# The first layer of a two-layer network as one stream of 64 pairs of heads, with every score formed twice and the softmax weights split on POOL and DVE

## The chip, the cores and the metric

The kernel runs on one core of a Trainium2 chip. Five engines share the work, each with its own queue of instructions in fixed order: PE (TensorE, matmuls and transposes, which write only to the eight PSUM banks), DVE (VectorE), ACT (ScalarE), POOL (GpSimd, which here touches only SBUF), and SP (SyncE), which issues the transfers. They meet through semaphores: an instruction waits until a counter has reached a value. The metric is the device time of one execution in microseconds (us), as the median of several.

## What is computed

Input x has 4 batches of 512 rows of 512 elements. Only the first layer (attention and a linear map, each with a layer norm before and after) is touched by the change; a second layer follows and stays as it is.

```
x = hidden_states                                   # (4, 512, 512), fp32
# first layer, attention: 32 heads of 16, one shared key and value head
n1 = layernorm(x);  q = n1 @ Wq;  k, v = n1 @ Wkv   # k, v: 16 wide
scores = q.k / 4 + slope[h] * (key_pos - query_pos), masked where key > query
x = x + layernorm((softmax(scores) @ v) @ Wo)
# first layer, linear map with 8-bit codes and scales
x = x + layernorm(layernorm(x) @ W.T + bias)
# then the second layer: attention with 32 heads of 128, and a gated feed-forward
```

## The kernel before

Products of fp32 data are formed from fp16 halves: a = hi + lo, and hi·hi + lo·hi + hi·lo is accumulated, so each use costs three matmuls, and each operand needs an instruction that makes hi (mostly ACT) and one that makes lo = a - hi (mostly DVE).

`layer0` works in rounds. `run(b, attend, back, front)` is one round: it attends batch b, carries the back part of batch b-1 (product with Wo, norms, linear map) and the front part of batch b+1 (norm and transposes). The rounds are run(-1) and run(4) without attention, run(0), a loop over run(1) and run(2), and run(3). Each ends with a barrier of all engines.

In a round the 32 heads go one at a time (h = 0..31). For head h, PE forms the scores of four tiles of 128 queries against the keys up to their own (1280 columns in all, `scores`, L459). DVE adds the distance bias from table `tab` and takes the row maximum in one instruction per tile (`biased`, L680), POOL makes `tab` for the head (L371), ACT exponentiates in SBUF (L575) with the row maximum as bias. PE then transposes the 10 blocks of weights (`transpose_probs`, L472), since the product with the values needs the keys on the partitions; ACT copies them to fp16 `pT_hi` (L543), DVE forms `pT_lo` (L708), and PE multiplies 10 blocks by the values in three terms (`weigh_values`, L484). A column of ones in the values gives the sum of each row, by which DVE divides at the start of the next round (L649, L652).

The order on PE is written out: in step h it transposes head h-1, stacks queries, weighs the values for head h-2, forms the scores of head h+1, and then does what `extra` puts there (products with Wq, Wo and the linear weights; transposes n1, n2, n3). The eight PSUM banks are a ring in the order of `uses`: a fill waits until the use eight places earlier has been emptied (`take`). On DVE step h is `biased_scores(h)`, then lo of the extras and of head h-1, then norms. The scores with bias lie in `xp`, four heads deep, and the fp16 weights three heads deep.

## Time and profile before

| | us |
|---|---|
| median of 3 runs | 2516.77 |
| lowest, highest | 2516.7, 2525.8 |
| profiled execution, its time | 2520.12 |
| profiled execution, span of the core | 2518.3 |

The profile is of one execution; its span starts with the first instruction and ends with the last, 1.8 us short of that execution's own time. The first layer lies from 58.97 us (DVE's first scalar) to 823.7 us (the last of its transposes is out). PE is busy 85% of the whole span, DVE 74%, ACT 61%, POOL 27%. A row of the form "L680 DVE ... x128 | 95.1, 743 | 4.3 <-PE" is a group: its line, engine and operation, what it writes and reads, how many; then its busy time in us and the mean ns of one; then the idle time before its members and what ended it. In a timeline a row has the start, the length (of all its members together where it says x4), and in brackets the idle time before it. PEclk in a stretch is the granted TensorE clock as a share of 2.4 GHz.

### The profile page before, as it was taken

How to read it: one execution, taken by the hardware profiler on the slowest of the kernel's cores; microseconds unless marked ns; L12 is line 12 of the kernel's file. 1: busy time of each engine (PE TensorE's matmuls, PEld its weight loads, DVE VectorE, ACT ScalarE, POOL GpSimd, SP SyncE). 2: the span in 40 equal slices, each digit the busy share in tenths (PEclk: the TensorE clock that was granted, in tenths of full speed). 3: DMA queues.
4: the chain of work that ended last, by engine and by line, in shares of the span. 5: the costliest groups of instructions: out<-in, count | busy, mean ns of one | idle time of the engine just before them, and what ended most of it. 6: DMA issues, size and time to landing. Idle time of an engine off the chain costs nothing. (4 is left out here: it accounts for less than half of the span.)

```text
span 2518.3 us, 49756 instructions
## 1 busy us (share of the span) xinstructions
PE 2146.9 (85%) x18352; PEld 1310.3 (52%) x18352; DVE 1864.5 (74%) x4645; ACT 1531.5 (61%) x3606; POOL 688.4 (27%) x563
## 2 busy tenths in 40 slices
PE   6688777778774589999999999999999999758997
PEld 2465555555552255555555555655555556423443
DVE  3688897897995477777777777777777777575554
ACT  2587776777771376667667676667666767341221
POOL 0312212111110243343433343334333333112221
PEclk9899899889997799999999999999999999978999
DMA  5101001000000343444334434443344333320000
GB/s 203 33 2 35 1 7 47 2 18 18 2 18 17 115 81 63 89 87 91 80 66 89 81 71 82 80 91 78 64 89 84 66 68 65 72 87 17 34 17 34
DMA packets 380593, 147.59 MB, mean 59 GB/s; under 512 B 354928, under 2 KB 359664, under 8 KB 378304
## 3 DMA queue, kind: packets, MB, share of 16 engines
q1 hardware_dynamic: 380352, 144.41, 25.5%
q8 instruction: 147, 2.41, 0.4%
q14 instruction: 94, 0.77, 0.1%
HBM read 48.95 MB, written 11.53 MB: 24 GB/s over the span
## 5 line engine op out<-in xcount | busy, mean ns | idle before, releaser
L1157 ACT ACTIVATE xp<-xp,nm 128x128 f32<-128x128 f32 (+3 forms) x512 | 281.3, 550 | 354.5 <-DVE nm L1236 354.5
L1017 POOL TENSOR_TENSOR q_in_sbuf<-q_in_sbuf,sinq 128x512 f32<-128x512 f32 x128 | 231.2, 1806 | 688.2 <-ACT q_in_sbuf L1145 581.3
L1207 DVE SCALAR_TENSOR_TENSOR probs_lo<-xp,rl,probs_hi 128x128 f16<-128x128 f32 (+3 forms) x512 | 263.5, 576 | 109.4 <-ACT probs_hi L1122 109.4
L575 ACT ACTIVATE xp<-xp,nm 128x512 f32<-128x512 f32 (+3 forms) x512 | 249.8, 569 | 50.9 <-DVE nm L680 49.1
L680 DVE CUSTOM_DVE_ANT_0 xp<-bank,tab,cs 128x512 f32<-128x512 f32 (+3 forms) x512 | 250.2, 545 | 4.3 <-PE bank L459 2.0
L1236 DVE CUSTOM_DVE_ANT_0 xp<-bank,mask,cs 128x128 f32<-128x128 f32 (+3 forms) x512 | 250.3, 545 | 0.0
L1122 ACT ACTIVATE probs_hi<-xp,rl 128x128 f16<-128x128 f32 (+3 forms) x512 | 244.0, 549 | 0.7 <-DVE rl L1256 0.7
L472 PE MATMUL bank<-ident,xp 128*128 128x128 f32 x1280 | 182.7, 291 | 62.6 <-ACT xp L575 45.6
L1041 PE MATMUL bank<-xT_hi,wq_hi 128*128 128x512 f16 x512 | 195.2, 381 | 43.2 <-DVE yacc L1251 37.4
L708 DVE TENSOR_TENSOR pT_lo<-bank,pT_hi 128x384 f16<-128x384 f32 (+1 forms) x384 | 207.1, 593 | 32.5 <-ACT pT_hi L543 32.4
L1041 PE MATMUL bank<-p1T_hi,v_hi 128*128 128x128 f16 x1280 | 223.0, 220 | 2.9 <-DMA p1T_lo<-probs_lo 2.9
L1041 PE MATMUL bank<-p1T_hi,v_lo 128*128 128x128 f16 x1280 | 222.9, 220 | 0.0
L1041 PE MATMUL bank<-p1T_lo,v_hi 128*128 128x128 f16 x1280 | 222.8, 220 | 0.0
L543 ACT ACTIVATE pT_hi<-bank 128x384 f16<-128x384 f32 (+1 forms) x384 | 181.0, 537 | 57.0 <-PE bank L472 55.0
L1024 POOL TENSOR_TENSOR qf<-q_in_sbuf,t 128x512 f32<-128x512 f32 x160 | 204.3, 1277 | 31.2 <-POOL q_in_sbuf L1017 19.0
L472 PEld LDWEIGHTS bank<-ident,xp 128*128 128x128 f32 x1280 | 150.4, 148 | 99.9 <-issue 27.9
L371 POOL TENSOR_SCALAR tab<-rel,cinv 128x512 f32<-128x512 f32 x128 | 92.5, 725 | 390.0 <-DVE nm L680 318.3
L1041 PE MATMUL bank<-xT_hi,wq_lo 128*128 128x512 f16 x512 | 195.2, 381 | 0.0
L1041 PE MATMUL bank<-xT_lo,wq_hi 128*128 128x512 f16 x512 | 195.0, 381 | 0.0
L1041 PE MATMUL bank<-wo_hi,o1T_hi 128*128 128x512 f16 x512 | 194.0, 379 | 1.1 <-issue 1.1
L1041 PE MATMUL bank<-wo_lo,o1T_hi 128*128 128x512 f16 x512 | 194.0, 379 | 0.0
L1041 PE MATMUL bank<-wo_hi,o1T_lo 128*128 128x512 f16 x512 | 194.0, 379 | 0.0
(235 smaller groups left out, 5535.9 us busy)
## 6 DMA issues: line engine op xcount, KB each, us to landing
raw_q<-in_wq SPq DMA_DIRECT2D x8, 1024.0 KB, 5.3
raw_o<-in_wo SPq DMA_DIRECT2D x8, 1024.0 KB, 5.6
x_front<-in_x SPq DMA_DIRECT2D x4, 1024.0 KB, 5.8
xb<-in_x SPq DMA_DIRECT2D x4, 1024.0 KB, 7.1
x_scratch<-xb SPq DMA_DIRECT2D x4, 1024.0 KB, 4.4
x_before<-x_scratch SPq DMA_DIRECT2D x4, 1024.0 KB, 5.6
wup<-in_wup SPq DMA_DIRECT2D x3, 1024.0 KB, 11.9
fused_scratch<-fused SPq DMA_DIRECT2D x12, 256.0 KB, 2.4
```

The source lines that it names most:

```text
L472: last = pe.transpose(bank[:, at:at + P], xp[:, h % 4, TRI[t] + j * P:TRI[t] + (j + 1) * P], C["ident"][:, :])
L543: act.activation(pT[0][:, h % 3, COLD[js[0]]:COLD[js[0]] + n, :], bank_of(("T", h, i))[:, 0:n * P].rearrange("p (t c) -> p t c", c=P), ACT ...
L575: act.activation(x, x, ACT.Exp, scale=-1.0, bias=nm[:, h % 4, t:t + 1]).then_inc(s_ex, 1)
L680: ins = dve.tensor_tensor_reduce(out=xp[:, h % 4, TRI[t]:TRI[t] + w], in0=bank_of(u)[:, at:at + w], in1=tab[:, h % 4, S - w:S], scale=cs[: ...
L708: dve.tensor_tensor(pT[1][:, h % 3, c, :], bank_of(u)[:, 0:n * P].rearrange("p (t c) -> p t c", c=P), pT[0][:, h % 3, c, :], ALU.subtract) ...
L1017: pool.tensor_tensor(qs[:, i % 2, :], qs[:, i % 2, :], rope["sink" if u[0] == "k" else "sinq"][:, :], ALU.mult).then_inc(s_rot, 1)
L1024: pool.tensor_tensor(qf[:, i % 2, :], qs[:, i % 2, :], t2[:, i % 2, :], ALU.add).then_inc(s_qf, 1)
L1041: ins = pe.matmul(out, lhs(a), rhs(c), start=(first and i == 0), stop=(last and i == 2))
L1122: ins = act.activation(pr[0][:, m % 2, c], xp[:, m % 3, c], ACT.Copy, scale=rl[:, m % 3, t:t + 1])
L1157: ins = act.activation(x, x, ACT.Exp, scale=-1.0, bias=nm[:, m % 3, t:t + 1], accum_out=ls[:, m % 3, t:t + 1])
L1207: ins = dve.scalar_tensor_tensor(pr[1][:, m % 2, c], xp[:, m % 3, c], rl[:, m % 3, t:t + 1], pr[0][:, m % 2, c], ALU.mult, ALU.subtract)
L1236: ins = dve.tensor_tensor_reduce(out=xp[:, m % 3, TRI[t]:TRI[t] + w], in0=bank_of(("s", m, i))[:, col:col + w], in1=mask[:, S - w:S], scal ...
```

## The change

The rounds go. All 4 x 16 = 64 pairs of heads pass through one stream of steps n, written out without a loop or a barrier; step n belongs to all engines.

- Scores are formed twice. A pair's scores go to five PSUM banks with queries on the partitions (`scores`, L544), only for their row maxima (`maximise`, five reductions on DVE). Six steps later they are formed again with keys on the partitions (`exponents`, L573), the maximum and the distance bias included as extra rows of the operands `q_stack` and `k_stack`, and ACT exponentiates straight from PSUM (`exponentials`, 5 x 128x512). So there is no transpose of weights, no `tab`, no `stack`. Blocks not computed or half masked are covered by matmuls of a constant (`mask_scores`, `mask_exponents`).
- The weights, 128x2560 fp32 for a pair in `px` (two deep), are split on POOL (`weights_hi`, one cast) and DVE (`weights_lo`, one subtraction). PE weighs the values in 40 small matmuls a pair.
- Queries are stacked by 24 transfers of 16x512 for every four pairs, maxima by 4 transfers, all issued by SP.
- Heads are normed on POOL (`norm_heads`, 16 small instructions for four pairs); the residual additions move from DVE to POOL (`add_rows`), the row norms from DVE and POOL to ACT (`normalise`).
- The other work hangs on steps: batch b's front and back parts lie in the steps that FRONT and BACK give, counted from 16b, and `others(n)` is filled at the end of PE's step n and emptied at the start of ACT's and DVE's step n+1.
- The banks stay one ring of eight, in the order of `fillings`.

```diff
+        X_LAG, V_LAG, N_LAG = 6, 8, 9
...
+        kz = sc.sb("k_stack_max", [P, 2, S], F16)
+        ks = sc.sb("k_stack", [P, 2, S], F16)
...
+        px = sc.sb("weights", [P, 2, 5, S])
+        ph = [sc.sb("weights_hi", [P, 2, 5, S], F16), sc.sb("weights_lo", [P, 2, 5, S], F16)]
...
+        STEPS = range(-16, NP + N_LAG + 20)
...
+        FRONT = {"load": -16, "stats": -13, "norm": -12, "n1": -10, "kv": -2}
+        BACK = {"load": 27, "o": 25, "y": (26, 27, 29, 30), "add1": 31, "n2": 33, "f": (34, 35, 37, 38),
+                "add2": 39, "n3": 42}
...
+        fillings = []
+        for n in STEPS:
+            if 0 <= n < NP:
+                fillings += [("s", n, i) for i in range(5)]
+            if 0 <= n - V_LAG < NP:
+                fillings.append(("pv", n - V_LAG))
+            if n % GP == 0 and 0 <= n // GP - 1 < NG:
+                fillings.append(("m", n // GP - 1))
+            if 0 <= n - X_LAG < NP:
+                fillings += [("x", n - X_LAG, i) for i in range(5)]
+            fillings += others(n)
+        place = {u: i for i, u in enumerate(fillings)}
...
+                def stack_queries(g):
+                    sp.wait_ge(s_qd, g + 1)
+                    if g >= GP:
+                        sp.wait_ge(*filled[("x", GP * (g - GP) + 3, 4)])
+                    else:
+                        sp.wait_ge(s_st, 2)
+                    for h in range(8):
+                        for lo, r in ((0, 16), (1, 32), (0, 48)):
+                            to = 64 * (h % 2) + r
+                            sp.dma_start(qs[to:to + E0, g % GP, h // 2, :],
+                                         qq[lo][h * E0:(h + 1) * E0, g % 2, :]).then_inc(s_qs[g % 2], 16)
...
+                def norm_heads(g):
+                    b, m = g // GP, g % GP
+                    pool.wait_ge(s_ro, g + 1)
+                    if m == 0 and b >= 1:
+                        pool.wait_ge(*last_of("o", b - 1))
+                    for h in range(8):
+                        c, o = (8 * m + h) * E0, ob[:, g % 2, h, :, :]
+                        if g or h:
+                            pool.wait_ge(s_on, 8 * g + h)
+                        pool.tensor_tensor(od[:, :, :], o[:, :, 0:E0], o[:, :, EV:EV + E0], ALU.add).then_inc(s_os, 1)
+                        pool.wait_ge(s_os, 8 * g + h + 1)
+                        pool.tensor_tensor(on[:, :, c:c + E0], od[:, :, :],
+                                           ro[:, g % 2, h, :].unsqueeze(2).to_broadcast([P, TT, E0]),
+                                           ALU.mult).then_inc(s_on, 1)
+                def weights_hi(p):
+                    pool.wait_ge(*emptied[("x", p, 4)])
+                    if p >= 2:
+                        pool.wait_ge(s_pf, p - 1)
+                    pool.tensor_copy(ph[0][:, p % 2, :, :], px[:, p % 2, :, :]).then_inc(s_wh, 1)
...
+                pool.wait_ge(s_sc, 1)
+                for n in STEPS:
+                    for u in norms_at(n):
+                        rstd(norm_no[u])
+                        if u in add_no:
+                            add_rows(u)
+                    if 0 <= n - X_LAG < NP:
+                        weights_hi(n - X_LAG)
+                    g, r = divmod(n - N_LAG - 3, GP)
+                    if r == 0 and 0 <= g < NG:
+                        norm_heads(g)
+
...
+                def take(u):
+                    i = place[u]
+                    if i >= 8:
+                        pe.wait_ge(*emptied[fillings[i - 8]])
+                    return banks[i % 8]
...
+                def mask_exponents(p):
+                    for i in range(5):
+                        out = take(("x", p, i))
+                        if i < 2:
+                            pe.matmul(out[:, 0:P], far[:, :], trit[:, 0, :], start=True, stop=False,
+                                      skip_group_check=True)
+                        else:
+                            parts = out[:, :].rearrange("p (a c) -> p a c", c=P)
+                            pe.matmul(parts[:, 0::3, :] if i < 4 else parts[:, 0::2, :], far[:, :], trit[:, :, :],
+                                      start=True, stop=False, skip_group_check=True)
+                def exponents(p):
+                    g, pp = p // GP, p % GP
+                    if pp == 0:
+                        pe.wait_ge(s_mr[g % 2], 16 * 4 * (g // 2 + 1))
+                        pe.wait_ge(s_kr, 2 * (g // GP) + 2)
+                    k = ks[:, g // GP % 2, :]
+                    for i, e, j, c in ((0, 0, 0, 0), (1, 1, 0, 0), (4, 0, 2, 0), (3, 1, 1, 0), (2, 0, 1, 0),
+                                       (3, 1, 3, 3 * P), (4, 1, 2, 2 * P), (2, 0, 3, 3 * P)):
+                        if (j, e) == (2, 1):
+                            pe.wait_ge(s_he, p + 1)
+                        r = slice(64 * e, 64 * (e + 1))
+                        ins = pe.matmul(bank_of(("x", p, i))[:, c:c + S - j * P], k[r, j * P:(j + 1) * P],
+                                        qs[r, g % GP, pp, j * P:S], start=False, stop=True, skip_group_check=True)
+                        if (j, e) == (2, 0):
+                            ins.then_inc(s_he, 1)
+                        elif j != 1:
+                            ins.then_inc(s_ef, 1)
...
+                    if 0 <= n < NP:
+                        mask_scores(n)
+                        scores(n)
+                    if 0 <= n - V_LAG < NP:
+                        weigh_values(n - V_LAG)
+                    if n % GP == 0 and 0 <= n // GP - 1 < NG:
+                        turn_maxima(n // GP - 1)
+                    if 0 <= n - X_LAG < NP:
+                        mask_exponents(n - X_LAG)
+                        exponents(n - X_LAG)
+                    for u in others(n):
+                        fill(u)
...
+                def exponentials(p):
+                    if p >= 2:
+                        act.wait_ge(s_wl, p - 1)
+                    for i in range(5):
+                        act.wait_ge(*filled[("x", p, i)])
+                        act.activation(px[:, p % 2, i, :], bank_of(("x", p, i))[:, :], ACT.Exp,
+                                       scale=unit[:, 0:1]).then_inc(s_ed, 1)
...
+                for n in STEPS:
+                    for u in others(n - 1):
+                        evacuate(u)
+                    for u in norms_at(n):
+                        normalise(u)
+                    if 0 <= n - X_LAG < NP:
+                        exponentials(n - X_LAG)
+                    if 0 <= n - V_LAG < NP:
+                        copy_heads(n - V_LAG)
...
+                def maximise(p):
+                    g, pp = p // GP, p % GP
+                    if g >= 2 and pp == 0:
+                        dve.wait_ge(*filled[("m", g - 2)])
+                    m4 = mx[:, g % 2, 0:32].rearrange("p (e a t) -> p e a t", e=2, t=TT)
+                    for i in range(5):
+                        bank = bank_of(("s", p, i))
+                        dve.wait_ge(*filled[("s", p, i)])
+                        if i < 2:
+                            ins = dve.tensor_reduce(m4[:, i, pp, 3:4], bank[:, :], AX.X, ALU.max)
+                        elif i < 4:
+                            ins = dve.tensor_reduce(mp[:, g % 2, GP * (i - 2) + pp, :],
+                                                    bank[:, :].rearrange("p (a c) -> p a c", c=P), AX.X, ALU.max)
+                        else:
+                            ins = dve.tensor_reduce(m4[:, :, pp, 1], bank[:, :].rearrange("p (a c) -> p a c", c=2 * P),
+                                                    AX.X, ALU.max)
+                        ins.then_inc(s_sd, 1)
+                def weights_lo(p):
+                    dve.wait_ge(s_wh, p + 1)
+                    dve.tensor_tensor(ph[1][:, p % 2, :, :], px[:, p % 2, :, :], ph[0][:, p % 2, :, :],
+                                      ALU.subtract).then_inc(s_wl, 1)
...
+                scalars()
+                for n in STEPS:
+                    if n % GP == 0 and 0 <= n // GP - 1 < NG:
+                        join_maxima(n // GP - 1)
+                    for u in others(n - 1):
...
+                    if 0 <= n - X_LAG - 1 < NP:
+                        weights_lo(n - X_LAG - 1)
+                    if 0 <= n < NP:
+                        maximise(n)
...
-        run(-1, False, False, True)
-        run(0, True, False, True)
-        with nc.Fori(1, B - 1) as b:
-            run(b, True, True, True)
-        run(B - 1, True, True, False)
-        run(B, False, True, False)
```

The first place is DVE's queue. Before, in a round's third step, the biased scores of one head (its second row, `nm`, is the row maximum of the same instruction), then the lo of an older head and of a query projection:

```order
L680 ISA xp,nm<-bank,tab,cs 128x512 [waits s_s_filled,s_table]
L680 ISA nm 128x1
L680 ISA xp,nm<-bank,tab,cs 128x384 [waits s_s_filled]
L680 ISA nm 128x1
L680 ISA xp,nm<-bank,tab,cs 128x128
L680 ISA nm 128x1
L708 TENSOR_TENSOR pT_lo<-bank,pT_hi 128x384 [waits s_t_hi_out] x2
L708 TENSOR_TENSOR pT_lo<-bank,pT_hi 128x512 [waits s_t_hi_out]
L644 TENSOR_TENSOR qT_lo<-bank,qT_hi 128x512 [waits s_s_hi_out]
```

And now, in step 32, with the emptying of a query projection and the statistics of the back part's rows ahead:

```order
L896 TENSOR_REDUCE mx<-mp 128x8 [waits s_scores_maximised]
L898 COPY mx<-mp 128x8 [waits s_dve_steps]
L856 SCALAR_TENSOR_TENSOR q_lo<-bank,fq,q_hi 128x512 [waits s_queries_hi]
L812 BN_STATS st<-xb 128x6 [waits s_rows_added] x4
L820 BN_AGGR mv<-st 128x2 [waits s_dve_steps,s_rows_normed]
L820 BN_AGGR mv<-st 128x2 x3
L822 TENSOR_SCALAR ve<-mv 128x4 [waits s_dve_steps]
L890 TENSOR_TENSOR weights_lo<-weights,weights_hi 128x2560 [waits s_weights_hi]
L879 TENSOR_REDUCE mx<-bank 128x1 [waits s_scores_filled,s_maxima_transposed]
L879 TENSOR_REDUCE mx<-bank 128x1 [waits s_scores_filled]
L881 TENSOR_REDUCE mp<-bank 128x4 [waits s_scores_filled] x2
L884 TENSOR_REDUCE mx<-bank 128x2 [waits s_scores_filled]
```

Where the lo followed the maxima of a newer head, the one lo of a pair (L890, waiting for POOL) now stands ahead of the five maxima of the pair seven steps younger.

The second place is PE's queue around the product with the values. Before, transposes, the stacking of queries, and the product:

```order
L472 MATMUL bank<-ident,xp 128x128 [waits s_exp,s_s_freed_by_dve]
L472 MATMUL bank<-ident,xp 128x128 x2
L472 MATMUL bank<-ident,xp 128x128 [waits s_exp,s_t_lo_out]
L472 MATMUL bank<-ident,xp 128x128 x3
L443 MATMUL bank<-qT_hi,sel 128x512 [waits s_s_freed_by_dve,s_t_lo_out]
L444 MATMUL bank<-qT_lo,sel 128x512
L484 MATMUL bank<-v,pT_hi 128x17 [waits s_t_lo_out]
```

Now, behind the product with the values of a pair:

```order
L555 MATMUL bank<-tri_T,far 128x128 [waits s_exponentials] x2
L559 MATMUL bank<-tri_T,far 128x2x128 [waits s_scores_maximised] x3
L573 MATMUL bank<-q_stack,k_stack 128x512 x2
L573 MATMUL bank<-q_stack,k_stack 128x256
L573 MATMUL bank<-q_stack,k_stack 128x384 x2
L573 MATMUL bank<-q_stack,k_stack 128x128
L573 MATMUL bank<-q_stack,k_stack 128x256 [waits s_half_of_exponents_filled]
L573 MATMUL bank<-q_stack,k_stack 128x128
L524 MATMUL bank<-tri,far 128x128 [waits s_scores_maximised] x2
L527 MATMUL bank<-tri,far 128x256 [waits s_pv_out]
```

The transposes are gone; the second forming of the scores (L573) stands behind mask fills (L559) that take banks from the maxima of this same step.

The third place is POOL. Before it made tables and, in rounds with a front part, normed four row tiles:

```order
L371 TENSOR_SCALAR tab<-rel,cinv 128x512 [waits s_s_freed_by_dve] x2
L359 TENSOR_TENSOR rs<-ve,mhalf 128x4 [waits s_variance]
L363 TENSOR_SCALAR x_front<-x_front,mv,rs 128x512 [waits s_rstd]
L363 TENSOR_SCALAR x_front<-x_front,mv,rs 128x512 x3
L371 TENSOR_SCALAR tab<-rel,cinv 128x512 [waits s_s_freed_by_dve] x6
```

Now, in the steps in which batch 0's rows are added:

```order
L458 TENSOR_TENSOR rs<-ve,mhalf 128x4 [waits s_rows_normed,s_variance]
L460 TENSOR_TENSOR nb<-mv,rs 128x4 [waits s_rstd]
L462 TENSOR_SCALAR nb<-nb 128x4 [waits s_rstd]
L491 TENSOR_TENSOR xb<-xb,yb 128x512 [waits s_rows_normed,s_x_loaded]
L491 TENSOR_TENSOR xb<-xb,yb 128x512 [waits s_rows_normed] x3
L483 CAST weights_hi<-weights 128x2560 [waits s_pv_filled,s_exponentials]
```

POOL used to work ahead of the heads; its cast now stands between ACT's exponentials and DVE's lo of every pair.

## Rows read from the trace of the kernel before

**Rows 1.** Stretches of the first layer: length, busy per engine, PEclk, DMA share, GB/s.

```profile
core 0: us, PE busy (x) PEld busy (x) DVE busy (x) ACT busy (x) POOL busy (x), PEclk, DMA share, GB/s
400.70:580.00 179.30, 142.49 (x1652) 100.50 (x1653) 157.15 (x452) 126.34 (x296) 34.16 (x39) 0.89 0.06 19
757.00:830.00 73.00, 33.70 (x170) 20.25 (x166) 39.52 (x81) 10.15 (x17) 4.04 (x4) 0.71 0.10 33
```

**Rows 2.** Waits from 400 to 579 us: waiter, who ended it, us, times, longest.

```profile
POOL tab L371 <- DVE nm L680: 78.5, 20, 16.2
...
ACT xp L575 <- DVE nm L680: 17.0, 8, 6.6
```

**Rows 3.** Groups on POOL, whole span.

```profile
L1024 POOL TENSOR_TENSOR qf<-q_in_sbuf,t 128x512 f32<-128x512 f32 x160 | 204.3, 1277 | 31.2 <-POOL q_in_sbuf L1017 19.0 <-DVE t L1223 7.6
L371 POOL TENSOR_SCALAR tab<-rel,cinv 128x512 f32<-128x512 f32 x128 | 92.5, 725 | 390.0 <-DVE nm L680 318.3 <-POOLq L96 69.4
...
L363 POOL TENSOR_SCALAR x_front<-x_front,mv,rs 128x512 f32<-128x512 f32 x12 | 24.8, 2082 | 0.3
...
L1826 POOL MEMSET mhalf<- 128x8 f32 x1 | 0.1, 105 | 0.3 <-POOLq L1940 0.3
```

**Rows 4.** Groups on DVE, whole span.

```profile
L680 DVE CUSTOM_DVE_ANT_0 xp<-bank,tab,cs 128x512 f32<-128x512 f32 x128 | 95.1, 743 | 4.3 <-PE bank L459 2.0 <-PE bank L472 1.4 <-POOL tab L371 0.7
L1215 DVE TENSOR_TENSOR q1T_lo<-qf,q1T_hi 128x512 f16<-128x512 f32 x128 | 87.6, 684 | 13.8 <-ACT q1T_hi L1136 13.6
...
L170 DVE TENSOR_TENSOR raw_wf<-raw_wf,qscales 128x2048 f32<-128x2048 f32 x1 | 2.3, 2293 | 0.0
L172 DVE TENSOR_REDUCE w_am<-raw_wq 128x1 f32<-128x2048 f32 x1 | 2.3, 2287 | 11.8 <-DMA raw_wq<-in_wq 11.8
```

**Rows 5.** DVE's timeline, first tens of microseconds.

```profile
14.00 0.74 DVE L172 TENSOR_REDUCE w_am<-raw_wkv 128x1 f32<-128x576 f32 x1
```

**Rows 6.** Groups on ACT, whole span.

```profile
L575 ACT ACTIVATE xp<-xp,nm 128x512 f32<-128x512 f32 x128 | 93.8, 733 | 47.7 <-DVE nm L680 47.7
...
L575 ACT ACTIVATE xp<-xp,nm 128x128 f32<-128x128 f32 x128 | 51.8, 405 | 0.0
...
L1560 ACT ACTIVATE silu_gate<-bank_g,tern_scale 128x512 f32<-128x512 f32 x40 | 27.5, 688 | 144.7 <-PE bank_g L1515 144.6
```

**Rows 7.** ACT's timeline, a head's four exponentials behind the copy of `stk`.

```profile
483.65 0.59 ACT L535 ACTIVATE stk<-bank 128x512 f16<-128x512 f32 x1
484.14 1.90 ACT L575 ACTIVATE xp<-xp,nm 128x512 f32<-128x512 f32 x4
```

**Rows 8.** PE's timeline: 128x512 matmuls at half clock, and later at full.

```profile
79.18 0.63 PE L398 MATMUL bank<-front_T_hi,wkv_lo 128*128 128x512 f16 x1
79.61 0.63 PE L398 MATMUL bank<-front_T_lo,wkv_hi 128*128 128x512 f16 x1
...
482.96 0.38 PE L443 MATMUL bank<-qT_hi,sel 128*128 128x512 f16 x1
483.17 0.38 PE L444 MATMUL bank<-qT_lo,sel 128*128 128x512 f16 x1
```

**Rows 9.** SP's timeline: two transfers of 64 KB issued.

```profile
844.81 1.23 SPq L1000 DMA_DIRECT2D raw_kv<-in_wkr  x2
```

**Rows 10.** DVE's timeline in the last round: first, some statistics, last.

```profile
758.73 0.95 DVE L649 RECIPROCAL rsum<-ob 128x128 f32<-128x128 f32 x1 [2.13 <-PEq L96]
...
776.49 2.47 DVE L592 BATCH_NORM_STATS2 st<-yb 128x6 f32<-128x512 f32 x4 [10.99 <-ACT yb L563]
...
822.98 0.69 DVE L639 TENSOR_TENSOR xT_lo<-bank,xT_hi 128x512 f16<-128x512 f32 x1 [0.16 <-ACT xT_hi L512]
```

**Rows 11.** Second layer's timeline: POOL's additions with DVE's subtraction beside them.

```profile
2271.30 6.03 POOL L1459 TENSOR_TENSOR yacc<-x_before,normed 128x512 f32<-128x512 f32 x4 [1.27 <-DVE normed L1593]
...
2271.81 1.31 DVE L1724 TENSOR_TENSOR hidden_lo<-hidden,hidden_hi 128x512 f16<-128x512 f32 x1
```

935 lines of the change are left out of this document (497 added, 438 removed).

## The prediction

> **What bounds the kernel now.** I read the stretches of the first layer first. A steady round is 179.3 us, that is 11.2 us for each of its 16 pairs of heads with everything else included. DVE is busy for 157.15 of it, PE for 142.49, ACT for 126.34, POOL for 34.16 [rows 1]. Then the waits of that stretch: POOL waits for DVE 78.5 us, ACT waits for DVE 17.0 [rows 2], while DVE, before its 128 biggest instructions, stood idle 4.3 us in all [rows 4]. So DVE sets the pace and the others work beside it, buffered three or four heads deep. The reader is to see two things: what takes work off DVE could pay, and 11.2 us a pair is the mark that the new stream has to beat. More exactly: the layer ends at 823.7 us. Its end in the new kernel is a start, 57 periods of the step, and a run-out. With start and run-out as worked out below, the new kernel breaks even at a period of 9.9 us.
>
> **What the change takes and adds, by load.** Off PE go the transposes and the stacking of queries, on comes the second forming of the scores with its masks, 3584 columns a pair: at the pace of 0.21 us for 512 columns [rows 8] that is 1.5 us; and the product with the values is 40 matmuls of 34 columns, 0.6 by columns. PE has room. ACT loses the copies of transposed weights and gets five exponentials of full width. DVE's load a pair becomes one lo of 2560 columns, five reductions and its share of the other work. By length, DVE's one row of this kind (2293 ns for 2048 columns, against 684 for 512) gives 1.05 ns a column, so 2.83 us; a reduction is 2287 ns for 2048 [rows 4] and 0.74 us for 576 [rows 5], so 0.673 us for 512, five make 3.37. The other work of a batch is some 20 emptyings and lo of 0.69, three statistics of 2.47 and some 0.5 [rows 10], and about 17 of keys, values, maxima and row sums: 39 us, 2.44 a pair. DVE's load is thus 8.6 us a pair, below 11.2. By load alone the change wins. The question is whether load or a chain of waits sets the step.
>
> **The chain of a step.** Read the order of the three engines together. In step n, DVE's queue has `weights_lo(n-7)` ahead of `maximise(n)`. PE's mask fills for `exponents(n-6)` take, in the ring of eight, the banks that stand eight places earlier: those of the pair's last ones are the first three score banks of pair n, the same step. So they wait for three reductions of `maximise(n)`. Behind the masks come the exponents, then ACT's five exponentials, then POOL's one cast, which waits for the fifth, then DVE's `weights_lo(n-6)`, which waits for the cast and stands ahead of `maximise(n+1)`. The circle closes in one step, and no buffer in it can get ahead: two deep in `px` doesn't help, since the exponents themselves wait for the maxima. The period is therefore the sum of the links:
>
> - PE, from the last maximum to ACT's first start: a mask and the first product. Before, ACT's copy of `stk` starts 0.69 us after PE's first of two matmuls of 512 columns at full clock [rows 7, 8]; at half clock these follow each other at 0.43 instead of 0.21 [rows 8], which makes 1.1 to 1.2. I take 0.9.
> - ACT, five of 128x512 from PSUM: such a one is 0.688; from SBUF 0.733 at 512 columns and 0.405 at 128 [rows 6]. The four of a head together (1280 columns) take 1.90 though their means sum to 2.28 [rows 6, 7]: each gives 0.12 back to overlap. 5 x 0.688 less 4 x 0.12 is 3.0.
> - POOL, a cast of 128x2560, fp32 to fp16, of one input. No row has such a cast. The nearest is `tab`, one input and 512 columns: 0.725 [rows 3]. A fixed part of 0.105, the smallest POOL row [rows 3], leaves 0.62 for 512; five of these and the fixed part are 3.2, I take 3.1. Upper bounds: the two-input product, 1.277 x 5 = 6.4, and the one-input row with two scalars, 2.08 x 5 = 10.4 [rows 3]. Lower: the slope of ACT's exponentials, (0.733 - 0.405) / 384 = 0.85 ns a column [rows 6], gives 2.3 with the fixed part, say 2.4. A gain is excluded, since the cast starts only when ACT's fifth is out and lo only when the cast is out. I stay at 3.1, since `tab` is nearest in kind.
> - DVE, lo of 2560 columns: 2.83. Then the three reductions: 2.02. In every fourth step the turned maxima take a bank of the ring and a fourth reduction counts: 0.17 on average.
> - Handing over between engines, five times beyond what the links hold: 0.15 in all.
>
> Sum: 0.9 + 3.0 + 3.1 + 2.83 + 2.02 + 0.17 + 0.15 = 12.2 us. PE's own work and ACT's emptyings fall into the 8.9 us of ACT, POOL and lo, and are hidden; if PE ran at half clock throughout, they would just fill it.
>
> The Trainium skill (GPSIMD Engine Reference, sections 3.1 and 4.1) says that an operation with one input is roughly at line rate on GpSimd, 1.03 cycles an element. The row of `tab` does not agree: 0.725 for 512 columns is well above. By that rule the cast would be an estimated 2.2 us and the period 11.3.
>
> **What comes on top of the chain.** Instructions in DVE's queue ahead of lo are free as long as they end before POOL's cast does: after the maxima DVE has the links of PE, ACT and POOL, 7.0 us, less the two last reductions, so some 5.7 us. Steps with little fit in. Those with emptyings, statistics of four row tiles (3 us) and reciprocals do not, because what they wait for arrives late or lies behind each other: of 16 steps, seven carry such work (n mod 16 = 0, 4, 7, 8, 11, 12, 15), with an excess of 1 to 3 us. Four batches: between 40 and 70 us, I take 55. The 24 transfers with which SP stacks queries for four pairs take 24 x 0.62 = 15 us by SP's row (two in 1.23) [rows 9] out of 49 for four steps, so they are hidden. Where POOL norms eight heads in 16 small instructions, it does so just beside lo. In the second layer a DVE subtraction of two SBUF operands beside POOL's additions took 1.31 [rows 11] against 0.684 in general [rows 4]. Lo lengthened by 0.34 to 0.9 of itself in 14 or 15 steps is 14 us. The sum on top: 69.
>
> The Trainium skill (SBUF — State Buffer, Who interferes with whom) says that a DVE instruction with two SBUF inputs contends with a GpSimd instruction that reads SBUF and that the later one waits for the whole of the other. The trace agrees with the contention (1.31 against 0.684). Lo mostly starts first; by that rule it would lose at most one small POOL instruction each time, and the 14 us would be about 5.
>
> **Start and run-out.** From 58.97: norm of batch 0 some 20 (with the load), transposes and first queries 8, the 24 transfers and their landing 17, six steps of scores alone at 5 reductions each, 3.4, so 20, and stacking the maxima 6: 71, first exponents at 130. After the last maxima the chain runs six pairs more without scores (6 x 5.5), the last heads are normed (8 x 3), and the back part of batch 3 follows. That back part took from 758.73 to 823.7 before, 65 [rows 10], at a PEclk of 0.71 [rows 1], and I take the same; part of the six pairs lies beside norming, so 33 + 24 + 65 = 122, with handing over 130.
>
> **The forecast.** 130 + 57 x 12.2 + 69 + 130 = 1024 us for the end of the layer, against 823.7: 200 us longer. The profiled execution's own 2520.12 becomes 2720.8; its median is 3.35 lower, so 2717. The second layer and the preparation are untouched.
>
> **Rivals.**
> (A) The chain as above, 2717; with the links off by 8% (56 us) and the extras by 20, 2640 to 2790. For it: the three orders; the row of `tab`. Chance 0.62.
> (B) The cast is dear, near the two-input rate: 3.3 us more in each period is 188, of which 40 come back because the extras then fit: 2865. At 10.4 for the cast it would be 3093. For it: the spread of POOL's rows between one shape and another (0.725 to 2.08). Against: `tab` is nearer in kind. Chance 0.15.
> (C) The cast at 2.4, PE's link 0.7 and extras of 42: a period of 11.3, end at 130 + 644 + 42 + 130 = 946, time 2639; with start and run-out each 20 shorter, 2600. Chance 0.13. The skill's rate for the cast, named above, would lead here.
> (D) Faster: the fills of the exponents do not in fact wait for the maxima of the same step, so that ACT and POOL get a pair ahead of DVE, and DVE's load of 8.6 us is the period: 130 + 57 x 8.65 + 130 = 753, time 2446. It decides where the mean step is below 9.9 us. Against it: the ring's order, which puts three score banks of the same step under the exponents' masks; DVE idle ahead of lo would have to be near nothing. Chance 0.07. That both nearly cancel (a mean step of 9.7 to 10.1) has 0.03.
>
> **How the numbers follow.** The likeliest is A, 2717. The range takes A, most of C and B up to its middle value: 2590 to 2860. Within 0.5%, about what a measurement of this kernel can tell from no change, 0.03; faster 0.07; slower 0.90, from A, B and C.
>
> **What would show it.** Of the changed kernel's profile: a steady step of some 13.4 us (12.2 and 1.2 of extras); POOL's cast at a mean near 3.1; DVE idle ahead of lo, ended by POOL, some 4 us a step, and DVE busy for 65% of the stream; PE's mask fills (L559) ended by DVE's reductions; ACT idle ended by PE; PEclk below the 0.89 of before. Wrong would be: the mask fills rarely waiting for DVE (then D), a cast beyond 5 us (B), or a start or run-out of 200 us instead of 130, which the first and last of L890 show at once.

## The result, and the profile after

The changed kernel takes 2711.65 us (median of 4 runs, 2706.31 to 2716.75) against 2520.28 of the kernel before. The ratio is 1.0757, with a 95% interval of 1.0725 to 1.0789. The forecast was 2717. The last transposes of the first layer are out at 1019.96 us instead of 823.67. From there to the end it is 1695.0 us, against 1694.6 before, so the second layer is what it was, and all but 0.4 of the 196.7 us that the span grew (2715.0 less 2518.3) lie in the first layer.

Its stretches, in the columns of [rows 1]: the start up to the first exponential, the first steps, the steady stream, and the steps without scores, then the last back part.

```profile
core 0: us, PE busy (x) PEld busy (x) DVE busy (x) ACT busy (x) POOL busy (x), PEclk, DMA share, GB/s
58.97:141.00 82.03, 36.51 (x213) 16.35 (x215) 42.37 (x110) 20.74 (x34) 4.96 (x42) 0.61 0.12 39
141.00:229.00 88.00, 54.04 (x527) 25.99 (x521) 49.75 (x59) 29.27 (x54) 25.75 (x24) 0.62 0.06 13
229.00:880.00 651.00, 433.72 (x3997) 211.67 (x3998) 382.06 (x523) 234.64 (x421) 268.83 (x295) 0.68 0.07 19
880.00:926.90 46.90, 27.13 (x324) 15.37 (x322) 26.77 (x23) 24.34 (x45) 27.89 (x29) 0.68 0.01 2
926.90:1021.00 94.10, 41.70 (x259) 26.09 (x257) 36.37 (x76) 29.95 (x47) 34.37 (x60) 0.71 0.09 34
```

In the steady stream no engine is near full: DVE 59%, PE 67%, ACT 36%, POOL 41%, where DVE had 88% in [rows 1]. The granted clock of PE is 0.68 instead of 0.89. Every engine has time to spare here, so they must be waiting for each other. The timeline of one step, all engines, shows that they do so in a circle. Columns are the start, the length, engine, line and tiles, and in brackets the idle time before and what ended it.

```profile
189.89 2.32 POOL L483 CAST weights_hi<-weights 128x2560 f16<-128x2560 f32 x1 [8.84 <-ACT weights L726]
...
192.24 2.83 DVE L890 TENSOR_TENSOR weights_lo<-weights,weights_hi 128x2560 f16<-128x2560 f32 x1 [5.34 <-POOL weights_hi L483]
...
194.99 1.28 DVE L879 TENSOR_REDUCE mx<-bank 128x1 f32<-128x512 f32 x2
...
195.73 0.39 PE L559 MATMUL bank<-tri_T,far 128*128 128x256 f16 x1 [2.14 <-DVE mx L879]
196.19 1.27 DVE L881 TENSOR_REDUCE mp<-bank 128x4 f32<-128x512 f32 x2
...
196.32 0.40 PE L559 MATMUL bank<-tri_T,far 128*128 128x256 f16 x1 [0.20 <-DVE mx L879]
...
196.92 0.39 PE L559 MATMUL bank<-tri_T,far 128*128 128x256 f16 x1 [0.20 <-DVE mp L881]
...
197.25 1.27 PE L573 MATMUL bank<-q_stack,k_stack 64*128 64x512 f16 x8
...
197.98 3.00 ACT L726 ACTIVATE weights<-bank,unit 128x512 f32<-128x512 f32 x5 [7.87 <-PE bank L573]
...
201.05 2.32 POOL L483 CAST weights_hi<-weights 128x2560 f16<-128x2560 f32 x1 [8.84 <-ACT weights L726]
...
203.40 2.83 DVE L890 TENSOR_TENSOR weights_lo<-weights,weights_hi 128x2560 f16<-128x2560 f32 x1
```

Read it from lo to lo: 192.24 lo, 194.99 maxima (2.75), 196.83 third maximum out (1.84), 197.98 exponentials (1.15), 201.05 cast (3.07), 203.40 lo (2.35): 11.16 us, and the links hardly overlap. Such a step, with nothing late ahead of lo, is called clean below. The three mask fills L559 each start right behind one of DVE's reductions: they are the link that the order of the ring makes. The waits of the whole stream (141 to 880 us: waiter, who ended it, us, times, longest) say the same in sums:

```profile
POOL weights_hi L483 <- ACT weights L726: 392.0, 53, 13.8
ACT weights L726 <- PE bank L573: 346.3, 47, 9.6
PEld bank L559 <- DVE mx L879: 133.2, 100, 3.3
...
DVE q_lo L856 <- ACT q_hi L701: 63.6, 13, 5.7
...
DVE weights_lo L890 <- POOL weights_hi L483: 52.4, 20, 5.3
```

POOL waits for ACT, ACT for PE, PE for DVE and DVE for POOL: in [rows 2] the arrows led to DVE only. The groups of the page give the sizes:

```profile
L726 ACT ACTIVATE weights<-bank,unit 128x512 f32<-128x512 f32 x320 | 191.7, 689 | 362.8 <-PE bank L573 362.8
...
L483 POOL CAST weights_hi<-weights 128x2560 f16<-128x2560 f32 x64 | 148.4, 2320 | 409.4 <-ACT weights L726 409.4
...
L890 DVE TENSOR_TENSOR weights_lo<-weights,weights_hi 128x2560 f16<-128x2560 f32 x64 | 183.8, 2871 | 65.1 <-POOL weights_hi L483 64.9
```

The 57 periods from the first lo (147.03) to the 58th (881.73) sum to 734.7 us, a mean of 12.89. Against 57 x 11.15 that leaves 99 us of extras. Followed step by step in the timeline, 79 of them lie between the end of the cast and the start of lo, in steps in which something late stands ahead of lo on DVE, as in this one, where PE forms queries and a tile of the linear map:

```profile
496.97 1.27 PE L573 MATMUL bank<-q_stack,k_stack 64*128 64x512 f16 x8
...
497.71 3.00 ACT L726 ACTIVATE weights<-bank,unit 128x512 f32<-128x512 f32 x5 [9.08 <-PE bank L573]
...
500.77 2.32 POOL L483 CAST weights_hi<-weights 128x2560 f16<-128x2560 f32 x1 [10.05 <-ACT weights L726]
...
501.94 0.69 ACT L701 ACTIVATE q_hi<-bank,fq 128x512 f16<-128x512 f32 x1 [0.94 <-PE bank L516]
...
502.66 0.75 DVE L856 SCALAR_TENSOR_TENSOR q_lo<-bank,fq,q_hi 128x512 f16<-128x512 f32 x1 [4.42 <-ACT q_hi L701]
...
504.53 0.75 DVE L865 SCALAR_TENSOR_TENSOR yb<-bank,gm,bias 128x512 f32<-128x512 f32 x1 [1.12 <-PE bank L516]
...
505.92 2.45 DVE L812 BATCH_NORM_STATS2 st<-x_front 128x6 f32<-128x512 f32 x4
...
508.97 2.82 DVE L890 TENSOR_TENSOR weights_lo<-weights,weights_hi 128x2560 f16<-128x2560 f32 x1
```

The cast is out at 503.1, yet lo starts at 508.97. DVE idled 4.42 us for the queries and 1.12 for the product, and then did the statistics that could have been done in the idle time, but stand behind it.

Another 16 us lie ahead of ACT's exponentials, in 11 steps like the next one:

```profile
509.14 3.54 POOL L458 TENSOR_TENSOR rs<-ve,mhalf 128x4 f32<-128x4 f32 x1 [6.05 <-DVE ve L822]
...
512.90 1.28 DVE L881 TENSOR_REDUCE mp<-bank 128x4 f32<-128x512 f32 x2
...
513.32 2.92 ACT L718 ACTIVATE x_front<-x_front,nb,rs 128x512 f32<-128x512 f32 x4 [10.69 <-POOL nb L462]
...
516.15 2.97 ACT L726 ACTIVATE weights<-bank,unit 128x512 f32<-128x512 f32 x5
```

POOL's row factor starts beside lo (508.97) and takes 3.54 us instead of the 1.04 that it takes alone (last section). ACT's row norm waits for it and stands ahead of the exponentials, which start 2.6 us behind the third maximum instead of 1.15. The remaining 4 us are small delays at the same place where the turned maxima take a bank.

### The profile page after: what moved, and what is told of

Its sections match the earlier page's. It is cut to its first block and busy times, and to the rows that moved or that the text cites. A ratio compares the mean times of both kernels' runs of the same rounds, so it can differ in the third digit from the quotient of the medians.

```text
span 2715.0 us, 44950 instructions
## 1 busy us (share of the span) xinstructions
PE 2167.9 (80%) x16896; PEld 1202.4 (44%) x16896; DVE 1761.9 (65%) x3602; ACT 1359.9 (50%) x3014; POOL 913.7 (34%) x851
## 5 line engine op out<-in xcount | busy, mean ns | idle before, releaser
L726 ACT ACTIVATE weights<-bank,unit 128x512 f32<-128x512 f32 x320 | 191.7, 689 | 362.8 <-PE bank L573 362.8
L483 POOL CAST weights_hi<-weights 128x2560 f16<-128x2560 f32 x64 | 148.4, 2320 | 409.4 <-ACT weights L726 409.4
L890 DVE TENSOR_TENSOR weights_lo<-weights,weights_hi 128x2560 f16<-128x2560 f32 x64 | 183.8, 2871 | 65.1 <-POOL weights_hi L483 64.9
L1224 PE MATMUL bank<-xT_lo,wq_hi 128*128 128x512 f16 x512 | 196.7, 384 | 0.0
L559 PE MATMUL bank<-tri_T,far 128*128 128x256 f16 x192 | 69.4, 373 | 127.1 <-DVE mx L879 111.0
L1224 PE MATMUL bank<-kT_hi,q1T_hi 128*128 128x128 f16 (+3 forms) x512 | 148.5, 303 | 18.9 <-DVE q1T_lo L1398 18.2
L1224 PE MATMUL bank<-kT_hi,q1T_lo 128*128 128x128 f16 (+3 forms) x512 | 154.9, 303 | 0.0
L1224 PE MATMUL bank<-kT_lo,q1T_hi 128*128 128x128 f16 (+3 forms) x512 | 154.8, 302 | 0.0
```

Source lines behind the costliest of these rows:

```text
L483: pool.tensor_copy(ph[0][:, p % 2, :, :], px[:, p % 2, :, :]).then_inc(s_wh, 1)
L559: pe.matmul(parts[:, 0::3, :] if i < 4 else parts[:, 0::2, :], far[:, :], trit[:, :, :], start=True, stop=False, skip_group_check=True)
L726: act.activation(px[:, p % 2, i, :], bank_of(("x", p, i))[:, :], ACT.Exp, scale=unit[:, 0:1]).then_inc(s_ed, 1)
L890: dve.tensor_tensor(ph[1][:, p % 2, :, :], px[:, p % 2, :, :], ph[0][:, p % 2, :, :], ALU.subtract).then_inc(s_wl, 1)
L1224: ins = pe.matmul(out, lhs(a), rhs(c), start=(first and i == 0), stop=(last and i == 2))
```

## The experiments

The first six alter one thing each in the changed kernel; those under the last heading build on the first of them. Times are medians; a ratio is to the kernel before, run beside it.

**Lo behind the maxima.** This takes lo and cast out of the circle and leaves every load as it is.

```diff
-                    if 0 <= n - X_LAG - 1 < NP:
-                        weights_lo(n - X_LAG - 1)
                     if 0 <= n < NP:
                         maximise(n)
+                    if 0 <= n - X_LAG - 1 < NP:
+                        weights_lo(n - X_LAG - 1)
```

> On DVE, the lo of pair n-7 goes behind the five maxima of pair n instead of ahead of them; nothing else changes. Theory of the circle (maxima of the same step, masks, exponents, exponentials, cast, lo, next maxima): POOL's cast and DVE's lo drop out of the circle, and the step is set by load. DVE's load in the changed kernel's steady stretch is 382 us for 50.5 steps, 7.6 a step, PE's 434, 8.6 a step at its granted clock of 0.68. With some waits a step of about 9 instead of 12.9: 57 x 3.9 = 222 us less, some 2490 us (2450 to 2560), under the kernel before. Rival (the loads themselves, PE at half clock and DVE sharing SBUF with POOL, set the step): within 20 us of 2712.

Measured: 2528.07 us, ratio 1.0013 (0.9999 to 1.0026). The rival of loads is out: the same instructions in another order give back 184 of the 191 us. The mean period is 9.51 us. Here is its stretch from 229 to 700 us:

```profile
229.00:700.00 471.00, 339.02 (x3830) 182.69 (x3830) 386.01 (x503) 224.52 (x407) 256.90 (x296) 0.81 0.09 24
```

DVE is busy for 82% and PE's clock rose to 0.81 by itself. The 82% is close to the 88% of [rows 1]. The time is 38 us above the theory's central figure (2490) and inside its range.

**Exponents first in PE's step and in the ring.** The masks of the exponents then wait for the maxima of the step before.

```diff
+            if 0 <= n - X_LAG < NP:
+                fillings += [("x", n - X_LAG, i) for i in range(5)]
             if 0 <= n < NP:
                 fillings += [("s", n, i) for i in range(5)]
...
+                    if 0 <= n - X_LAG < NP:
+                        mask_exponents(n - X_LAG)
+                        exponents(n - X_LAG)
                     if 0 <= n < NP:
                         mask_scores(n)
                         scores(n)
```

> PE does the masks and exponents of pair n-6 at the start of step n, ahead of the scores of pair n, and the ring of banks has the same order; DVE's order stays (lo ahead of the maxima). The exponents' banks then come from the maxima of step n-1. Circle theory: the circle spans two steps, so it no longer binds, as in the run with lo behind: 2450 to 2580. Rival (it is DVE's order of lo before maxima that costs, whatever the ring does, or the loads): 2690 to 2720.

Measured: 2578.12 us, ratio 1.0203 (1.0183 to 1.0223). DVE's order is untouched, and still 134 us are gone: the circle needs both lo ahead of the maxima and the maxima ahead of the same step's exponents. Cut at either place it opens. The time is at the upper end of what was expected, and its waits from 300 to 750 us show what is left:

```profile
PEld bank L527 <- ACT weights L726: 102.5, 25, 11.1
```

The score masks now take banks that ACT's exponentials of the same step must empty, which is another circle.

**The cast twice.**

```diff
+                    pool.tensor_copy(ph[0][:, p % 2, :, :], px[:, p % 2, :, :]).then_inc(s_w2, 1)
+                    pool.wait_ge(s_w2, p + 1)
                     pool.tensor_copy(ph[0][:, p % 2, :, :], px[:, p % 2, :, :]).then_inc(s_wh, 1)
```

> POOL casts each pair's weights twice, the second over the first, and only the second signals DVE: 2.4 us more a pair. Circle theory: POOL's cast is a link of every step in which DVE has nothing late ahead of its lo. By the list of the 57 periods, the steps above 11.15 us that do not end in a wait for POOL have slack, and what is left is 78 us more: 2790 (2770 to 2810). If POOL's cast were hidden: 2712. If it were on the path of every step: 2850.

Measured: 2809.72 us, 98 more than the changed kernel. The 57 periods sum to 813.3 us against 734.7: 79 more, where the slack counted step by step gave 78. The estimate had left out the last six pairs, where the cast has no cover: from the 58th lo to the layer's end it is 9 us more, and the start gives 1. That makes 88 in the layer (1108.12 against 1019.96). Of the other 10 between the medians, 5 are there because the profiled execution of the changed kernel (2716.75) lies that much above its median, and 4.6 lie behind the first layer, a stretch that takes between 1693 and 1700 us in these profiles. So the cast is on the path in a part of the steps, neither hidden (0) nor always exposed (137).

**The cast in five pieces**, each as soon as its exponential is out.

```diff
-                    pool.wait_ge(*emptied[("x", p, 4)])
                     if p >= 2:
                         pool.wait_ge(s_pf, p - 1)
-                    pool.tensor_copy(ph[0][:, p % 2, :, :], px[:, p % 2, :, :]).then_inc(s_wh, 1)
+                    for i in range(5):
+                        pool.wait_ge(*emptied[("x", p, i)])
+                        pool.tensor_copy(ph[0][:, p % 2, i, :], px[:, p % 2, i, :]).then_inc(s_wh, 1)
```

> POOL casts the five banks of a pair one by one, each as soon as its exponential is out; DVE's lo waits for the fifth. Circle theory: the link between ACT's last exponential and lo shrinks from 2.32 to about 0.55 us, which counts only in the 20 or so steps in which DVE waits for POOL ahead of lo (at most 1.8 each, 31 us by the list of the waits), and in those up to the time at which the emptyings come: 2680 (2665 to 2700). If the cast is not on the path: 2712.

Measured: 2682.66 us, 29 less. The clean step is 9.4 instead of 11.15, a gain of 1.8 as expected. But only some 20 of 57 steps are clean, and the others had lost their wait for POOL already: the periods sum to 703.8, 31 less. This is the same link measured from the other side.

**Useless matmuls that keep PE busy.**

```diff
                         out = take(("s", p, i))
+                        if i == 0 and not others(p - 1):
+                            for _ in range(10):
+                                pe.matmul(out[:, :], far[:, :], oner[:, :], start=True, stop=False,
+                                          skip_group_check=True)
...
                         out = take(("x", p, i))
+                        if i == 0:
+                            for _ in range(8):
+                                pe.matmul(out[:, :], far[:, :], oner[:, :], start=True, stop=False,
+                                          skip_group_check=True)
```

> The changed kernel, with useless matmuls of 128x512 on PE, in banks that it is about to fill anyway: 10 ahead of the score masks in steps that follow no other product, 8 ahead of the exponents' masks, so that PE is not idle there; nothing of the result changes. Tests what the half clock (0.68 granted on average) is worth. Theory: PE's link in the circle goes from 1.15 to some 0.85 us and products of 12 matmuls end up to 2.5 us earlier for the emptyings that stand ahead of lo: a clock of 0.85 or more and 25 to 60 us less, 2650 to 2690. Rival (the clock costs nothing, PE has slack): 2712, or more where the added matmuls are in the way.

Measured: 2685.63 us, 26 less, at the near edge of what was expected; by the ratio to the kernel before, run beside each, it is 33 less (1.0624 against 1.0757). Its steady stretch and PE's link of a clean step:

```profile
229.00:880.00 651.00, 510.36 (x4771) 260.96 (x4772) 400.55 (x538) 248.15 (x450) 288.34 (x317) 0.91 0.07 20
```

```profile
184.70 1.27 DVE L889 TENSOR_REDUCE mp<-bank 128x4 f32<-128x512 f32 x2
...
184.84 0.28 PE L567 MATMUL bank<-tri_T,far 128*128 128x256 f16 x1 [0.31 <-DVE mx L887]
...
185.44 0.28 PE L567 MATMUL bank<-tri_T,far 128*128 128x256 f16 x1 [0.32 <-DVE mp L889]
...
185.66 0.84 PE L581 MATMUL bank<-q_stack,k_stack 64*128 64x512 f16 x8
...
186.17 3.00 ACT L734 ACTIVATE weights<-bank,unit 128x512 f32<-128x512 f32 x5 [7.54 <-PE bank L581]
```

At a granted clock of 0.91 instead of 0.68, from the third maximum (185.34) to ACT's start is 0.83 us instead of 1.15, and the clean step is 10.8. That is 0.3 in each of 57 steps, 17 or 18 us, of the 34 by which the sum of the periods fell (700.2). The rest fits products that end earlier, but wasn't measured apart. So the low clock is mostly a result of the waiting, as the clock of 0.81 with lo behind shows too; by itself it costs about 1%.

**Lo ahead of the emptyings.**

```diff
                         join_maxima(n // GP - 1)
+                    if 0 <= n - X_LAG - 1 < NP:
+                        weights_lo(n - X_LAG - 1)
                     for u in others(n - 1):
                         evacuate(u)
...
-                    if 0 <= n - X_LAG - 1 < NP:
-                        weights_lo(n - X_LAG - 1)
                     if 0 <= n < NP:
```

> The changed kernel, with DVE's lo ahead of the emptyings and statistics of its step instead of behind them, still ahead of the maxima. Tells whether the extras of some steps are work of DVE or its waiting for products of PE and ACT's halves. Steps without such work stay at 11.15. If it is mostly waiting, lo covers it: 20 to 60 us less. If it is mostly DVE work that found room while POOL was casting, that work now lies behind lo in the open: some 137 us of it against 99 of extras, 2730 to 2760. I expect the second, weakly.

Measured: 2729.6 us (two executions), at the lower edge of the second expectation. That is 18 more by the medians, but 11 by the ratio (1.0802 against 1.0757), and the periods sum to 738.3 against 734.7, only 4 more. Clean steps stay at 11.2. This fits work that now lies open behind lo in place of waits that lo now covers, which no run took apart. Between the two orders little is to be had; both put everything into one circle. As evidence on the extras it is weak, since both readings gave sums near this one.

**Versions on the way to a faster one.** All have lo behind the maxima. The first puts ACT's copy of the heads ahead of its exponentials.

```diff
-                    if 0 <= n - X_LAG < NP:
-                        exponentials(n - X_LAG)
                     if 0 <= n - V_LAG < NP:
                         copy_heads(n - V_LAG)
+                    if 0 <= n - X_LAG < NP:
+                        exponentials(n - X_LAG)
```

> As the run with lo behind the maxima, and ACT copies the heads of pair n-8 ahead of the exponentials of pair n-6 instead of behind them. In the run with lo behind, PE waited 87 us (of 300 to 750) for that copy before it could mask the next scores, so a smaller circle is left: exponentials, copy, masks and scores of the next pair, maxima, exponents; its clean step is 7.9. Theory: the copy (0.42) and its place behind 3.0 us of exponentials leave the circle, steps shorten by some 0.4 to 1 us: 2505 to 2485 against 2528. Rival (DVE's load of 82% busy already sets the step): 2520 to 2530.

Measured: 2521.41 us, ratio 0.998 (0.9971 to 0.9989). It gave 7 us, where the theory said 23 to 43: the time is the rival's (2520 to 2530). In its waits (300 to 700 us) the next small instruction shows:

```profile
PE bank L527 <- DVE m_lo L902: 26.3, 9, 3.0
```

The second takes ACT's row norms behind the exponentials and POOL's additions behind the cast.

```diff
-                    for u in norms_at(n):
-                        normalise(u)
                     if 0 <= n - V_LAG < NP:
                         copy_heads(n - V_LAG)
                     if 0 <= n - X_LAG < NP:
                         exponentials(n - X_LAG)
+                    for u in norms_at(n):
+                        normalise(u)
...
                     for u in norms_at(n):
                         rstd(norm_no[u])
-                        if u in add_no:
-                            add_rows(u)
                     if 0 <= n - X_LAG < NP:
                         weights_hi(n - X_LAG)
+                    for u in norms_at(n):
+                        if u in add_no:
+                            add_rows(u)
```

> As the run with the copy first, and besides ACT's row norms stand behind the exponentials of their step, and POOL's row additions behind its cast (POOL's small norm instructions stay ahead of it). With lo behind the maxima, ACT waited 63 us (of 300 to 750) for POOL's norm factors ahead of the exponentials, in 11 of the steps. Theory: those waits leave the exponentials' path, 20 steps by 1 to 3 us each: 20 to 40 us under the run with the copy first, if the norms are not in turn late for the next step's transposes. Rival: the same or slower, since the wait only moves to the next step's emptyings.

Measured: 2530.12 us, ratio 1.0012 (1.0001 to 1.0024): 9 slower than without this edit, so the rival (the same or slower) came true. That the wait only moved is its reading.

The third lets all small emptyings go first: on ACT also the high half of the maxima, on DVE their low half ahead of lo.

```diff
                         copy_heads(n - V_LAG)
+                    if n % GP == 0 and 0 <= n // GP - 1 < NG:
+                        maxima_hi(n // GP - 1)
                     if 0 <= n - X_LAG < NP:
                         exponentials(n - X_LAG)
...
                         maximise(n)
+                    if n % GP == 0 and 0 <= n // GP - 1 < NG:
+                        maxima_lo(n // GP - 1)
                     if 0 <= n - X_LAG - 1 < NP:
                         weights_lo(n - X_LAG - 1)
```

> Lo behind the maxima, and of each step all small instructions that empty a bank of the ring come first: on ACT the copy of heads and the high half of the maxima ahead of the exponentials, on DVE the low half of the maxima ahead of lo. In the run with the copy first PE waited 26 us (of 300 to 700) for that low half, behind lo, in 9 of the steps. Theory: 16 such steps by 1 to 3 us, 15 to 40 us less than 2521: 2480 to 2506. Rival: DVE's load of 82% already sets the step, and it comes out within 6 us of 2521.

Measured: 2520.09 us, ratio 0.9986 (0.9977 to 0.9995). Nothing that can be told was gained over the copy first: the time is the rival's. Its stretch and its groups from 229 to 700 us show why:

```profile
229.00:700.00 471.00, 343.03 (x3771) 182.60 (x3769) 389.24 (x499) 230.55 (x408) 257.20 (x297) 0.79 0.09 24
```

```profile
L890 DVE TENSOR_TENSOR weights_lo<-weights,weights_hi 128x2560 f16<-128x2560 f32 x49 | 152.8, 3119 | 25.4 <-POOL weights_hi L483 25.4
```

DVE is at 83%, and a lo takes 3.12 us on average instead of 2.87 in the changed kernel: part of DVE's busy time is waiting for POOL, as the last section shows. And DVE is still idle for 82 of these 471 us. Its longest waits in sum are:

```profile
DVE weights_lo L890 <- POOL weights_hi L483: 25.4, 10, 4.7
DVE back_T_lo L826 <- ACT back_T_hi L677: 22.7, 12, 7.2
DVE m_lo L902 <- ACT m_hi L741: 18.0, 7, 5.1
```

So DVE's share of 83% alone doesn't make it the bound.

On top of this, useless matmuls, and the cast in pieces:

> As the run with the small ones first, with useless matmuls of 128x512 on PE, 6 ahead of the score masks in steps behind no product and 3 ahead of the exponents' masks. Where the whole circle bound, full clock was worth 26 us. Here PEclk is 0.80 and DVE's load is closer to setting the step, so I expect less: 5 to 20 us under the run with the small ones first. Rival: the added matmuls lie in the way of the scores now that the steps are shorter, 0 to 20 us more.

> As the run with the small ones first, with POOL's cast in five pieces. In the whole circle this saved 29 us. With lo behind the maxima the cast has a step of time: theory says within 6 us of the run with the small ones first, since POOL is in no circle any more. Rival (POOL is still on the path): 20 us or more less.

Measured: 2522.09 us, ratio 0.9996 (0.9984 to 1.0008), and 2521.92 us, ratio 0.999 (0.998 to 0.9999). Neither moves the time by 0.1%, though the first raised the clock from 0.79 to 0.86. Both had been worth 1% while the circle was closed. The expected 5 to 20 us of the first did not come; that the cast in pieces brings nothing was as the theory had it. But the second says something on the bound too. Its stretch from 229 to 700 us:

```profile
229.00:700.00 471.00, 344.73 (x3703) 182.17 (x3700) 368.73 (x496) 228.73 (x404) 343.42 (x482) 0.79 0.09 24
```

DVE is busy for 20 us less than without the pieces (78% instead of 83%), and the time is the same. So DVE's busy time as the profile counts it doesn't set the time either. POOL's busy time rose from 257 to 343 us meanwhile, so part of the blocking may only have moved from DVE's side to POOL's. What binds these last versions stays open.

## Why the prediction was right

The forecast was 2717 and the time is 2712, but four terms of the sum were off and cancelled.

- **The circle** was named as it is: the timeline shows it link by link, and it opens at either of the two places at which it was said to be closed.
- **The link of POOL** was too dear: 3.1 us forecast from `tab` [rows 3], 2.32 measured, 0.8 too much in each step. The 0.62 us for 512 columns belong to an instruction with a scalar operation. The cast runs at 0.9 ns a column, near ACT's slope of [rows 6], which was taken as the lower bound. The Trainium skill (GPSIMD Engine Reference, sections 3.1 and 4.1) has one-input operations at about line rate, by which the cast was an estimated 2.2 us: the trace agrees with the page and not with my choice.
- **The other links**: the reductions and lo start before the one ahead has ended, 1.84 and 2.75 instead of 2.02 and 2.83; ACT 3.07 with handing over; PE 1.15 instead of 0.9, since its clock fell to 0.68. Clean step 11.15 instead of 12.2. Over 57 steps this is 60 us too much; 10 of them are the forecast's 0.17 for the turned maxima, which no clean step holds and which the measured extras hold instead.
- **The extras** were 99 us instead of 69. POOL's small instructions beside lo were put at the wrong place: 14 us forecast on lo, some 1 measured there (2.91 instead of 2.82 in one step of four). But the row factor waits for lo in its turn, and with ACT's row norm behind it that reaches the exponentials in 11 steps. An estimate from the timeline is 5 to 12 us: without the wait they would start 0.85 or 1.4 us earlier, and in the steps of 1.4 other late work mostly holds lo back anyway. The forecast had nothing for this. The other work had 55 us in seven steps of 16. The seven hold 71, and the other nine, for which it had only the 0.17, hold 28. Most of the extras are waiting (read from the timeline; no run took it away alone): DVE's emptyings wait for products that PE forms, partly at half clock, after the exponents, and statistics that are ready queue behind them.
- **Start and run-out**: the first exponential came at 141.1 instead of 130, and from the last of the 57 periods to the layer's end were 144 us instead of 130, 25 us too little.

Sum: -60 + 30 + 25 = -5 us, which is the difference between forecast and result. The range was right for what the terms allowed; that the middle was hit is luck. Of the signs named, PE's mask fills waited for DVE's reductions as said, but DVE's idle time ahead of lo that POOL ended was 52.4 us in 20 steps, 0.9 a step and not 4, since mostly other late work stood there; DVE was busy for 59%, not 65%. Rival C had the step right (11.3) and missed by its extras of 42 and by the same start and run-out.

**Rival D**, load alone, was wrong for this kernel, and it holds only in part for the runs with lo behind. There the steps are under the 9.9 us that it named, but its number (2446) is still 74 us below the best of them: DVE is busy for 7.5 to 7.9 us a step and the mean period is 9.4 to 9.6, and the first exponential comes at 137 to 141 us there too, not at 130.

## What to carry to other kernels

Before trusting a sum of loads, follow one item's chain through all queues and look where it re-enters: an instruction that waits for a late partner (lo for the cast) placed ahead of one that starts the next item (the maxima) turns buffers of any depth into none. A ring of banks adds such arrows without any line of code that says so; write down, for each fill, whose emptying it waits for. Put the instruction that starts the next item and the small ones that free a bank ahead of the large one, then measure again before going on: a faster clock and an earlier cast were each worth 1% in the circle and nothing with it open. A busy share of 80% doesn't name the bound by itself, since it can hold time in which DVE waits for POOL (lo at 3.12 instead of 2.87 us).

## What the runs showed of the hardware

**A subtraction of two SBUF operands on DVE and POOL's instructions don't run side by side; the later one waits.** In the changed kernel POOL's small norm instructions take 0.3 us, except the one that starts beside lo (411.68 to 414.59 on DVE). POOL's timeline:

```profile
411.61 0.30 POOL L473 TENSOR_TENSOR od<-ob 128x64 f32<-128x64 f32 x1
411.99 2.75 POOL L475 TENSOR_TENSOR heads_normed<-od,ro 128x64 f32<-128x64 f32 x1
414.82 0.30 POOL L473 TENSOR_TENSOR od<-ob 128x64 f32<-128x64 f32 x1
```

The second row starts behind lo's start and ends when lo does. POOL's row factor (minimum, median and maximum in ns) takes 1.04 us alone and mostly 3.54 here; it is fed by the instruction ahead of lo and so starts right behind lo's start:

```profile
L458 POOL TENSOR_TENSOR rs<-ve,mhalf x20: 1037/3539/3651, 79.7 to 1012.4; 128x4 f32<-128x4 f32 x20
```

The Trainium skill (SBUF — State Buffer, Who interferes with whom) says that the later one blocks for the whole of the other. The trace agrees in both directions. Where lo starts first, POOL loses it all, which corrects my price from [rows 11], and 2.5 us on a row factor of 1.04 can lie on the path, as in the step at 509. In the run-out it is the other way round, from POOL's and DVE's timeline:

```profile
902.59 4.58 POOL L483 CAST weights_hi<-weights 128x2560 f16<-128x2560 f32 x2
...
904.93 4.91 DVE L890 TENSOR_TENSOR weights_lo<-weights,weights_hi 128x2560 f16<-128x2560 f32 x1 [4.38 <-POOL weights_hi L483]
```

The second cast ends at 907.17, and lo at 909.84, 2.7 us later: it took nearly its whole 2.8 us from the cast's end, though the profile has it begun, and busy, since 904.93. DVE's copy of 128x8 from SBUF (L898) shows the same in the run with the small ones first: 0.18 us at 214.5, 2.15 at 402.2, just behind the start of a cast at 402.0.

**A cast from fp32 to fp16 of 128x2560 on POOL took 2.32 us**, 0.9 ns a column, against 0.725 us for 512 columns of a one-input instruction with a scalar operation, 1.4 ns a column [rows 3]. Price by operation, not by the number of inputs alone.

**The granted clock follows how busy PE is kept.** It was 0.89 in the round before, 0.68 in the circle, 0.81 with the circle open, and 0.91 with useless matmuls in the same circle.
